# Four masked copies of k by ScalarE in place of GpSimd's product, and a later place for two PE steps, in a 24-pass attention pipeline

## The reference

```
q = x Wq + bq ;  k = src Wk + bk ;  v = src Wv + bv
scores[b,h] = q[b,:,h] k[b,:,h]^T / sqrt(8) (+ mask)
out = softmax(scores) v ;  y = x + out Wo + bo
```

## Time and profile before

| what | value |
|---|---|
| median of 3 runs | 506.92 us (505.62 to 507.88) |
| the profiled execution's own time | 506.91 us |
| its span, first to last instruction | 505.0 us |
| mean granted PE clock | 0.976 of full speed |
| PE, DVE, ACT, POOL busy | 450.8, 376.1, 298.8, 273.8 us |

### The profile page before, as it was taken

How to read it: one execution, slowest core, us unless ns; L and a number is a source line. 1 busy time by engine, 2 the same in 40 slices (tenths; PEclk the granted TensorE clock), 3 DMA queues, 4 the chain that set the end, 5 groups by cost and what they waited for, 6 DMA issues and landing times.

```text
span 505.0 us, 16946 instructions
## 1 busy us (share of the span) xinstructions
PE 450.8 (89%) x6872; PEld 358.2 (71%) x6872; DVE 376.1 (74%) x918; ACT 298.8 (59%) x724; POOL 273.8 (54%) x332
## 2 busy tenths in 40 slices
PE   4798899999999999898877688999999999999885
PEld 4466666766666667687766477887888888878674
DVE  6699868688988888877487874869777677767542
ACT  2377676677777776756653536555665556553441
POOL 6464877579867778955233643545354545431210
PEclk9799999999999999999899797999999999999999
DMA  8960000000000000000000000000000000000000
GB/s 280 241 229 3 2 3 3 2 3 3 1 4 3 2 4 3 3 0 2 1 1 2 3 1 2 2 13 3 12 3 1 13 3 12 1 13 3 14 1 21
DMA packets 12420, 11.54 MB, mean 23 GB/s; under 512 B 5176, under 2 KB 10296, under 8 KB 12344
## 3 DMA queue, kind: packets, MB, share of 16 engines
q1 hardware_dynamic: 11624, 9.01, 6.5%
q10 hardware_dynamic: 720, 1.45, 0.9%
HBM read 9.42 MB, written 1.05 MB: 21 GB/s over the span
## 4 chain that ended last, share of the span: by engine, by line
PE 49%; DVE 24%; issue 14%; POOL 7%; ACT 4%; DMA 1%; DVEq 0%; POOLq 0%; ACTq 0%
DVE negm L1245 8%; PE ps L732 5%; PE ps L616 5%; DVE blocks L1236 5%; PE ps L446 4%; PE ps L632 4%; PE ps L654 4%; PE ps L464 3%; PE ps L609 2%; PE ps L755 2%; PE ps L624 2%; PE ps L494 2%; PE ps L662 2%; PE ps L406 2%; PE ps L407 2%
## 5 line engine op out<-in xcount | busy, mean ns | idle before, releaser
L1245 DVE TENSOR_REDUCE negm<-ps 128x8 bf16<-128x512 f32 x96 | 59.6, 682 | 25.2 <-PE ps L446 25.1
L831 ACT ACTIVATE p<-ps 128x512 f32<-128x512 f32 x96 | 54.5, 595 | 28.3 <-PE ps L454 27.2
L837 ACT ACTIVATE shared<-ps 128x512 f32<-128x512 f32 x96 | 57.0, 601 | 21.6 <-PE ps L464 20.2
L1731 POOL TENSOR_TENSOR wide<-wide,cv 128x1024 f32<-128x1024 f32 x24 | 45.7, 1903 | 32.5 <-ACT wide L821 32.5
L464 PE MATMUL ps<-cst,p 128*128 128x128 f32 x384 | 58.5, 276 | 0.4 <-ACT shared L837 0.4
L1658 POOL TENSOR_TENSOR rstd<-veps,neghalf 128x2 f32<-128x2 f32 x40 | 29.3, 733 | 49.3 <-DVE veps L1281 30.5
L1784 POOL TENSOR_TENSOR probs<-p,rc 128x512 f32<-128x512 f32 x32 | 33.0, 1046 | 39.8 <-DVE rc L1531 39.7
L464 PEld LDWEIGHTS ps<-cst,p 128*128 128x128 f32 x384 | 44.2, 141 | 11.5 <-issue 9.4
L1026 ACT ACTIVATE late<-ps 128x512 f32<-128x512 f32 x32 | 17.3, 594 | 33.5 <-PE ps L755 33.5
L632 PE MATMUL ps<-wo,late 128*128 128x128 f32 x256 | 32.9, 284 | 3.1 <-ACT late L1026 3.1
L632 PEld LDWEIGHTS ps<-wo,late 128*128 128x128 f32 x256 | 32.4, 200 | 4.7 <-issue 4.0
(11 more groups left out here) (202 smaller groups left out, 1155.8 us busy)
## 6 DMA issues: line engine op xcount, KB each, us to landing
late<-in_mask_l SPq DMA_DIRECT2D x2, 512.0 KB, 10.8
result<-x_all SPq DMA_DIRECT2D x8, 128.0 KB, 1.8
x_all<-in_x_tok SPq DMA_DIRECT2D x1, 768.0 KB, 6.3
wide<-in_ctx_t SPq DMA_DIRECT2D x1, 768.0 KB, 7.7
rv<-in_rv ACTq DMA_DIRECT2D x1, 768.0 KB, 8.6
wa<-in_wa SPq DMA_DIRECT2D x1, 512.0 KB, 8.3
w<-in_w SPq DMA_DIRECT2D x2, 256.0 KB, 7.7
wq<-in_wq SPq DMA_DIRECT2D x1, 512.0 KB, 7.3
```

The source lines that it names most:

```text
L831: A_(p3[:, n % 3, :], ps[:, S_BANK[r], :], ACT.Exp, scale=SC8).then_inc(sm["act_exp"], 1)
L837: A_(pt[:, w % 2, r, :], pt_bank(RG * w + r), ACT.Copy).then_inc(sm["act_pt"], 1)
L1245: V.tensor_reduce(negm[:, n % 4, :], ps[:, S_BANK[r], :].rearrange("p (a k) -> p a k", k=S), AX.X, ALU.max, negate=True).then_inc(sm["dve_ ...
L1731: P.tensor_tensor(r_op[:, w % 2, :, :], k_t[:, w % 2, :].unsqueeze(1).to_broadcast([128, 4, GT]), head_masks.unsqueeze(2).to_broadcast([12 ...
```

## The change

POOL's product `mask_k` and the buffer `k_t` go. ACT writes the four masked copies of k straight from PSUM, each as `mask * k + mask * bk`, with the mask column as `scale` and a column of the new small tensor `bkm` as `bias`; the copy of q comes after them. `bkm` is made once at the start by three small products on POOL. On PE, "in" moves behind t1, and "out" behind t2.

```diff
-        k_t = wide[:, 6144:6656].rearrange("p (a k) -> p a k", a=2)
+        bkm = sb("bkm", [128, NPH, 4])
...
             def scores(w):
-                pe.wait_ge(sm["pool_k"], w + 1)
+                pe.wait_ge(sm["act_k"], 4 * (w + 1))
...
                 transpose_probs(w, 0)
+                transpose_probs(w, 1)
                 if w + 2 < NW:
                     transposes_in(w + 2)
-                transpose_probs(w, 1)
                 if w in (VIS, VIS + 1):
                     pooled_visual(w - VIS)
+                transpose_probs(w, 2)
                 if older:
                     project_out(w - 2)
-                transpose_probs(w, 2)
                 if w + 2 < NW:
                     project_qk(w + 2)
...
             def evac_qk(w):
                 act.wait_ge(sm["pe_qk"], w + 1)
-                if w >= 2:
-                    act.wait_ge(sm["pool_k"], w - 1)
-                A_(k_t[:, w % 2, :], a_bank(w)[:, GT:2 * GT], ACT.Identity, bias=col(f"bk{w // NG}")).then_inc(sm["act_k"], 1)
+                if w == 0:
+                    act.wait_ge(sm["bk_set"], NPH)
                 if w >= 2:
                     act.wait_ge(sm["pe_s"], w - 1)
+                for c in range(4):
+                    A_(r_op[:, w % 2, c, :], a_bank(w)[:, GT:2 * GT], ACT.Identity, bias=bkm[:, w // NG, c:c + 1],
+                       scale=head_masks[:, c:c + 1]).then_inc(sm["act_k"], 1)
                 A_(q_t[:, w % 2, :], a_bank(w)[:, 0:GT], ACT.Identity, bias=col(f"bq{w // NG}")).then_inc(sm["act_q"], 1)
...
-            def mask_k(w):
-                pool.wait_ge(sm["act_k"], w + 1)
-                if w >= 2:
-                    pool.wait_ge(sm["pe_s"], w - 1)
-                P.tensor_tensor(r_op[:, w % 2, :, :], k_t[:, w % 2, :].unsqueeze(1).to_broadcast([128, 4, GT]),
-                                head_masks.unsqueeze(2).to_broadcast([128, 4, GT]), ALU.mult).then_inc(sm["pool_k"], 1)
...
             pool.wait_ge(sm["ld_small"], 32)
-            mask_k(0)
-            mask_k(1)
+            for ph in range(NPH):
+                P.tensor_tensor(bkm[:, ph, :], head_masks, col(f"bk{ph}").to_broadcast([128, 4]), ALU.mult)\
+                    .then_inc(sm["bk_set"], 1)
...
-                if w + 2 < NW:
-                    mask_k(w + 2)
```

More of the change, by code:

```diff
@@ L238, in build @@
             ln0_mv ln0_ve ln0_r ln0 m_bias m3_split
-            pe_in act_in pe_qk act_q act_k pool_k pe_v dve_v pe_s dve_max pe_sm act_exp pe_pt act_pt pe_pv dve_ot
+            pe_in act_in pe_qk act_q act_k bk_set pe_v dve_v pe_s dve_max pe_sm act_exp pe_pt act_pt pe_pv dve_ot
             dve_rc dve_atok dve_at pe_o pool_res dve_y dve_st dve_mv dve_ve pool_r pool_yn pool_yg pool_x
```

## The result

| | before | after |
|---|---|---|
| median | 506.27 us (4 runs) | 513.25 us (512.6 to 515.7, 4 runs) |
| span of the profiled execution | 505.0 us | 511.6 us |
| ratio to before | | 1.016, 95% interval 1.012 to 1.020 |

The change costs 7.0 us (1.4% by the medians). The forecast was 515.5 us, +8.6.

A forecast was written before the change was run, and what follows sets the result against it. The prediction took the cycle of a pass as the bound: passes 1 to 7 +2.7, passes 8 to 21 +5.7, pass 22 +0.4, start -0.2, together +8.6, 515.5 us. Likeliest range 510.5 to 519; later given as 509 to 519.

The forecast's parts named there:

- Bound: One pass read as a cycle between first copies of k: 7.95 us in pass 17, head 2.62 and tail 5.33.
- Price of a copy: ACT's masked copies of k with bias and scale: 0.47 us each from start to start, bounds 0.37 and 0.56.
- side estimate with 0.49 us a copy: Skill's cost rule for a two-operand copy on ACT: 0.49 us start to start, sum some 1.5 us higher; not used.
- Plain head: First copy of k to L478, without extra ACT work: 3.12 us, as v's projection waits for q's copy.
- Head with squares: Passes 13 to 20, squares between q's copy and t3's copy on ACT: 0.44 us above the plain head.
- Tail: L478 to the next cycle: 5.2 us against 5.33, t2 waiting for ACT's copy of t0; gain 0.13 a pass.
- POOL: Without the product L1731, four passes stretched 0.1 to 1 us by POOL become like their neighbours.
- Start: Up to the first passes: three small POOL products and longer copies taken as 0 (-1 to +1), pass 0's moves -0.2 us.
- Cheap copies: Rival: ACT's masked copies cost 0.37 us each, head 2.75, +1 us, 508 us; chance 0.09.
- Hidden copies: Rival: ACT's copies issue every 0.32 us or less and stay hidden, PE's moves pay: -4.8, 502 us; chance 0.09.
- Dear copies: Rival: ACT's copies don't overlap, 0.56 us each, or lateness runs through ACT's queue: +8, 523 us; chance 0.07.

The follow-up runs named there:

- the split kernel: Changed kernel's PE order, but ACT masks k from k_t in SBUF behind q's copy, two of four copies behind the first exponential: 499.2 us, 0.986 of the kernel before.

## Why the prediction was right

**Bound.** Right: the cycle of a pass, not the shares of the page. ACT's 30 us more of work came out as 7 us, through one wait on L415 (0.75 to 0.89 us in attention 0, 0.21 in attention 1, 0.43 in attention 2) and one queue in front of L839.

**Price of a copy.** Right in form, a little high: 0.45 us from start to start, not 0.47. The removal of one operand (0.36) shows both the price and that the copies are on the path. The prediction's side estimate with 0.49 us a copy would add 0.02 x 4 x 22 = 1.8 us to its sum, not some 1.5.

**Plain head.** Forecast 3.12, measured 3.21. q's copy came earlier than forecast (1.81 for 1.88), but from L415 to L478 it took 0.86 (78.17 to 79.03 in pass 7) in place of 0.72. The two errors partly cancel; the plain cycle is 8.37 for 8.32.

**Head with squares.** This term was mis-sized: forecast 3.56, measured 3.42. The squares take 0.59 from start to ACT's next instruction (162.90 to 163.49), not the 0.69 read as start to end of the last, and the copies are 0.07 shorter. 8 passes x 0.19 us of cycle (8.76 to 8.57) is 1.5 us, the largest part of what the forecast was high by (1.6 us by the medians, 2.0 by the spans); the start (0.5 too high) and the plain cycles (0.05 too low each) nearly cancel.

**Tail.** Right: 5.16 for 5.2, with t2 released by ACT's copy of t0 as forecast. Within it two small errors cancel, which is luck: t2 comes 3.18 us behind L478 for 3.10, and t2 and out take 0.46 and 0.45 us to the next step for 0.50 and 0.52. But the reference was wrong: it was set against the tail of the kernel before (5.33), as a gain of 0.13. Against what the copies alone give (4.74 in pass 17) the move is a loss of 0.42 us in such a pass, and of 0.1 to 0.4 in the plain ones. The sum came out right, since it was made from the cycle after the change; the attribution did not. Of the 7 us, the copies are some 0.5 us (507.3 against 506.7 for the kernel before, timed beside it) and the moved steps the rest, while each edit alone is harmless or a gain. Counted the other way round, the moved steps gain 3.4 us in passes 1 to 21 and the copies then cost 10.4 (167.68 to 178.06): the loss belongs to the pair. The prediction had the copies as the whole cost. It also said that out "used to fill that time" in the kernel before. It did, at 171.19, but with little to spare, as DVE's transpose had ended at 171.04:

```profile
170.32 0.72 DVE L1253 STREAM_TRANSPOSE o_t<-ps 128x512 f32<-128x512 f32 x1
```

Once t1 has left the place ahead of out, out waits for that transpose, as the kernel with only "in" moved shows.

**POOL.** Passes 5, 6, 14 and 16 fell to the length of their neighbours as forecast. But in this kernel that is not POOL's merit: with the product put back, their cycles are the same. In passes 5 and 6 the residual waits 1.78 us for POOL there and the longer heads cover it; in passes 14 and 16 the instruction of L1281 is not held for long beside the product (0.50 us at most in the passes). In the changed kernel it (L1283 there) never took longer than 0.41 us. The prediction also put the excess of the four passes over their neighbours at 0.1 to 1 us; it was 0.6 to 1.4 (pass 5: 9.04 against 7.62).

**Start.** -0.7 us for -0.2. The three products take 0.55 us together, not up to 2.2, and DVE's norm (L1210, before L1208), which stood beside POOL's product before, took 0.59 us for 2.17. ACT's second input copy started at 14.49 for 15.22.

**Rivals.** Cheap copies: refuted by the 0.45; their forecast of the head (2.75) is near what copies with one operand gave (2.84). Hidden copies: refuted for this order; what that rival wanted is nearly reached by splitting them (0.15 us short in passes 17 to 20). Dear copies: refuted.

## What to carry to other kernels

Idle share says how much work an engine could take, and the place in its queue says whether it may: four copies (1.8 us) ahead of the copy that the next matmul waits for lengthen every head, while one copy more a pass, with two of the four moved into the wait behind the first exponential, costs 0.15 us or less in nearly every pass. Two edits to one cycle are to be costed together and each alone, since an order that is the best of those tried when DVE is late (out behind t2, -3.4 us in the passes) is the worst when the long heads give DVE time (+7.0 us). And when a bank is shared, ask first which copy frees it.

## What the runs showed of the hardware

Each column operand of an activation costs time: 128x256 from PSUM, start to start, 0.28 us with none (L814, 166.12 to 166.40 in the kernel with moved squares), 0.36 with a bias column, 0.45 with bias and scale. From SBUF with a scale column alone it was 0.40 ((159.67 - 158.87) / 2 in the split kernel); whether the source or the kind of operand makes the difference to 0.36 is open.

The part of the program behind the passes varies by itself. Two executions with the same instructions there, the changed kernel and the one with the squares moved, took 292 and 288 us for it:

```profile
219.00:511.00 292.00, 260.62 (x3702) 221.47 (x3702) 203.14 (x469) 156.90 (x420) 118.81 (x148) 0.97 0.02 6
```

```profile
217.00:505.00 288.00, 256.02 (x3702) 217.21 (x3702) 203.36 (x472) 157.09 (x421) 118.92 (x148) 0.99 0.02 6
```

The columns are the stretch, its length, busy time of PE, PEld, DVE, ACT and POOL, and the granted clock: 0.97 and 0.99 of full speed. The difference goes with stretches at half clock (1.2 in place of 2.4 GHz): the changed kernel has three behind the passes, the other one. Windows inside the three, and inside the one:

```profile
249.50:252.00 2.50, 2.50 (x14) 2.50 (x13) 0.00 (x0) 2.09 (x6) 0.00 (x0) 0.50 0.00 0
287.00:293.00 6.00, 5.12 (x73) 3.47 (x76) 4.72 (x14) 3.45 (x16) 3.08 (x4) 0.50 0.01 3
311.00:317.00 6.00, 5.45 (x19) 4.93 (x20) 1.81 (x5) 2.81 (x8) 2.04 (x2) 0.50 0.01 3
```

```profile
283.00:289.00 6.00, 4.42 (x48) 2.78 (x52) 4.71 (x13) 2.85 (x13) 3.15 (x4) 0.50 0.01 3
```

From 25 to 210 us the clock was 1.00 in both. What lowers it behind the passes was not tried. For a change to the passes, the cycles of one trace tell more than the times of single executions, which carry these 4 us.
